# Moving GpSimd's share of the layer normalisation to other periods, with statistics in two places

## The reference

```python
xn = _layernorm(x, axis=-1)
# attention on xn
Q = jnp.einsum('bnd,hdk->bhnk', x, proj_q)
K = jnp.einsum('bmd,dk->bmk', x, proj_k)
V = jnp.einsum('bmd,dv->bmv', x, proj_v)
logits = jnp.einsum('bhnk,bmk->bhnm', Q, K)
weights = jax.nn.softmax(logits, axis=-1)
O = jnp.einsum('bhnm,bmv->bhnv', weights, V)
Y = jnp.einsum('bhnv,hdv->bnd', O, proj_o)
# feed-forward on xn, summed over 8 experts: (xn @ w1[e]) @ w2[e]
x = x + Y + ffn
```

## Time and profile before

| | |
|---|---|
| median of 3 runs | 1669.72 us (1669.16 to 1669.86) |
| the profiled execution's own time | 1669.67 us |
| its span, first to last instruction | 1667.9 us |
| TensorE busy | 1634.7 us, 98% |
| ScalarE, VectorE busy | 1304.2 us (78%), 1239.3 us (74%) |
| GpSimd busy | 1379.9 us, 83% |
| mean granted clock of TensorE | 0.998 of full speed |
| bytes moved by DMA | 16.73 MB, mean 10 GB/s |

### The profile page before, as it was taken

The page is one execution under the profiler, slowest core; times in us unless marked ns, Lnnn a source line. Parts: engine busy times, 40 slices in busy tenths (PEclk is TensorE's granted clock), DMA queues, the critical chain, the costliest instruction groups (busy, mean ns, idle before and its releaser), DMA issues.

```text
span 1667.9 us, 46510 instructions
## 1 busy us (share of the span) xinstructions
PE 1634.7 (98%) x18820; PEld 1214.1 (73%) x18820; DVE 1239.3 (74%) x2655; ACT 1304.2 (78%) x1350; POOL 1379.9 (83%) x1008
## 2 busy tenths in 40 slices
PE   7999999999999999999999999999999999999998
PEld 6777777777777777777777777777777777777775
DVE  5777777777777777777777777777777777777775
ACT  4777877787787788778778777877878787787785
POOL 2788888888888888888888888888888888878876
PEclk9999999999999999999999999999999999999999
DMA  8000000000000000000000000000000000000000
GB/s 230 2 2 2 1 2 14 2 2 2 2 15 2 2 2 3 13 2 2 2 8 8 2 2 1 8 8 2 2 2 8 8 2 2 2 14 2 2 1 14
DMA packets 16769, 16.73 MB, mean 10 GB/s; under 512 B 432, under 2 KB 12976, under 8 KB 16560
## 3 DMA queue, kind: packets, MB, share of 16 engines
q1 hardware_dynamic: 15520, 13.24, 2.7%
q10 hardware_dynamic: 1040, 0.52, 0.1%
HBM read 9.57 MB, written 4.19 MB: 8 GB/s over the span
## 4 chain that ended last, share of the span: by engine, by line
POOL 56%; issue 24%; PE 18%; ACT 1%; DVE 0%; POOLq 0%; DMA 0%; SPq 0%; DVEq 0%; ACTq 0%
POOL pr_lo L306 40%; POOL xacc L318 9%; POOL xn L300 3%; PE s_ps L548 2%; PE s_ps L550 2%; PE s_ps L535 2%; PE t_ps L586 2%; PE t_ps L589 2%; PE t_ps L588 2%; POOL rstd L345 2%; POOL xacc L324 1%; POOL xn_lo L290 1%; PE s_ps L432 1%; PE s_ps L434 1%; PE s_ps L433 1%
## 5 line engine op out<-in xcount | busy, mean ns | idle before, releaser
L306 POOL TENSOR_TENSOR pr_lo<-pr,pr_hi 128x1024 f16<-128x1024 f32 x511 | 1086.4, 2134 | 264.3 <-ACT pr_hi L396 264.3
L389 ACT ACTIVATE pr<-s_ps,boost,scale 128x1024 f32<-128x1024 f32 x512 | 616.8, 1205 | 211.1 <-PE s_ps L550 210.3
L778 DVE TENSOR_REDUCE key_max<-s_ps 128x128 f16<-128x1024 f32 x512 | 624.0, 1219 | 0.0
L396 ACT ACTIVATE pr_hi<-pr 128x1024 f16<-128x1024 f32 x512 | 525.4, 1051 | 8.1
L548 PE MATMUL s_ps<-g_lo,xT 128*128 128x128 f16 x4096 | 512.4, 219 | 1.1 <-DVE g_lo L791 1.1
L550 PE MATMUL s_ps<-g_hi,xT 128*128 128x128 f16 x4096 | 512.3, 219 | 0.0
L548 PEld LDWEIGHTS s_ps<-g_lo,xT 128*128 128x128 f16 x4096 | 400.7, 98 | 31.6 <-DVE g_lo L791 1.6
L550 PEld LDWEIGHTS s_ps<-g_hi,xT 128*128 128x128 f16 x4096 | 400.8, 98 | 29.7
L586 PE MATMUL t_ps<-pr_hi,xn_hi 128*128 128x512 f16 x1024 | 388.7, 380 | 16.3 <-POOL pr_lo L306 14.4
L588 PE MATMUL t_ps<-pr_lo,xn_hi 128*128 128x512 f16 x1024 | 388.1, 379 | 0.0
L589 PE MATMUL t_ps<-pr_hi,xn_lo 128*128 128x512 f16 x1024 | 388.1, 379 | 0.0
(11 more groups left out here) (123 smaller groups left out, 1602.7 us busy)
## 6 DMA issues: line engine op xcount, KB each, us to landing
out_dram<-xacc SPq DMA_DIRECT2D x16, 256.0 KB, 2.3
w_sb<-in_L_ffn_w_dram SPq DMA_DIRECT2D x1, 2048.0 KB, 10.2
pr<-in_L_attn_proj_q_dram ACTq DMA_DIRECT2D x1, 512.0 KB, 4.7
xacc<-in_L_attn_x_dram SPq DMA_DIRECT2D x2, 256.0 KB, 5.1
pr<-in_L_attn_proj_o_dram SPq DMA_DIRECT2D x1, 512.0 KB, 6.5
xacc<-in_L_attn_x_dram SPq DMA_DIRECT2D x1, 384.0 KB, 11.0
xacc<-in_L_attn_x_dram SPq DMA_DIRECT2D x1, 128.0 KB, 6.3
wkv<-in_L_attn_proj_k_dram SPq DMA_DIRECT2D x1, 64.0 KB, 2.9
```

Source lines behind the costliest of these rows:

```text
L306: pool.tensor_tensor(pr_lo[:, u % RING, :], pr32[:, u % PR, :], pr_hi[:, u % RING, :], ALU.subtract)\
L389: act.activation(pr32[:, u % PR, :], both_banks(u), ACT.Exp, bias=boost[:, 0:1], scale=scale[:, 0:1])\
L396: act.activation(pr_hi[:, u % RING, :], pr32[:, u % PR, :], ACT.Copy).then_inc(p_hi_ready, 1)
L778: dve.tensor_reduce(key_max[:, u % 2, :], both_banks(u).rearrange("p (t q) -> p q t", q=P), AX_X, ALU.max).then_inc(keys_max, 1)
```

## The change

The statistics get two slots, used in turn by even and odd tiles (`ln_slot`). VectorE's three steps stay in periods 0, 1 and 3 of pair p for tile p + 10. GpSimd and ScalarE now do their steps for that tile one pair later, in pair p + 1: `pow` in period 0 (before: 2), the normalisation in period 1 (before: 3), the high half on ScalarE in period 3 (before: 6), the low half in period 5 (before: 7). VectorE's wait before `bn_aggr` is for one normalised tile less. When TensorE turns the tile is unchanged.

```diff
@@ sizes: AHEAD + 1 becomes AHEAD + 2 for stats, mean_var, var_eps, rstd @@
+        def ln_slot(tile):
+            return AHEAD + tile % 2
...
@@ GpSimd @@
-                pool.tensor_scalar(xn32[:, 0, 1:D], xacc[:, tile, 1:D], mean_var[:, AHEAD, 0:1],
-                                   rstd[:, AHEAD:AHEAD + 1], ALU.subtract, ALU.mult).then_inc(ln_xn32, 1)
+                slot = ln_slot(tile)
+                pool.tensor_scalar(xn32[:, 0, 1:D], xacc[:, tile, 1:D], mean_var[:, slot, 0:1],
+                                   rstd[:, slot:slot + 1], ALU.subtract, ALU.mult).then_inc(ln_xn32, 1)
...
-                if n % 8 == 2 and (tile := ln_tile(n // 8)) is not None:
-                    pool.wait_ge(ln_var, tile - AHEAD + len(FIRST_TILES) + 1)
-                    pool.tensor_tensor(rstd[:, AHEAD:AHEAD + 1], var_eps[:, AHEAD:AHEAD + 1],
-                                       minus_half[:, 0:1], ALU.pow).then_inc(ln_rstd, 1)
-                if n % 8 == 3 and (tile := ln_tile(n // 8)) is not None:
-                    normalise_next(tile)
-                if n % 8 == 7 and (tile := ln_tile(n // 8)) is not None:
-                    xn_low(tile, 0, 1)
+                if (tile := ln_tile(n // 8 - 1)) is not None:
+                    if n % 8 == 0:
+                        slot = ln_slot(tile)
+                        pool.wait_ge(ln_var, tile - AHEAD + len(FIRST_TILES) + 1)
+                        pool.tensor_tensor(rstd[:, slot:slot + 1], var_eps[:, slot:slot + 1], minus_half[:, 0:1], ALU.pow)\
+                            .then_inc(ln_rstd, 1)
+                    if n % 8 == 1:
+                        normalise_next(tile)
+                    if n % 8 == 5:
+                        xn_low(tile, 0, 1)
@@ ScalarE @@
-                if n % 8 == 6 and (tile := ln_tile(n // 8)) is not None:
+                if n % 8 == 3 and (tile := ln_tile(n // 8 - 1)) is not None:
                     split_high(tile, 0, 1)
@@ VectorE: bn_stats, bn_aggr and the addition of EPS use ln_slot(tile); and @@
-                    dve.wait_ge(ln_xn32, tile)
-                    tile_mean(AHEAD)
+                    dve.wait_ge(ln_xn32, tile - 1)
+                    tile_mean(ln_slot(tile))
```

More of the change, by code:

```diff
@@ L66, in attention_ffn @@
         xn32 = sb("xn32", [P, AHEAD, D], F32)
[L67 to L70, removed]
+        stats = sb("stats", [P, AHEAD + 2, 6], F32)
+        mean_var = sb("mean_var", [P, AHEAD + 2, 2], F32)
+        var_eps = sb("var_eps", [P, AHEAD + 2], F32)
+        rstd = sb("rstd", [P, AHEAD + 2], F32)
         minus_half = sb("minus_half", [P, AHEAD], F32)
@@ L861, in before_bias @@
                         dve.wait_ge(x_in[4], 16)
-                    dve.bn_stats(stats[:, AHEAD, :], xacc[:, tile, :]).then_inc(ln_stats, 1)
+                    dve.bn_stats(stats[:, ln_slot(tile), :], xacc[:, tile, :]).then_inc(ln_stats, 1)
                 if at == 1 and (tile := ln_tile(pair)) is not None:
                     dve.wait_ge(ln_stats, tile + 1)
-                    dve.wait_ge(ln_xn32, tile)
-                    tile_mean(AHEAD)
+                    dve.wait_ge(ln_xn32, tile - 1)
+                    tile_mean(ln_slot(tile))
                 if at == 3 and (tile := ln_tile(pair)) is not None:
                     dve.wait_ge(ln_mean, tile + 1)
-                    dve.tensor_scalar_add(var_eps[:, AHEAD:AHEAD + 1], mean_var[:, AHEAD, 1:2], EPS).then_inc(ln_var, 1)
+                    slot = ln_slot(tile)
+                    dve.tensor_scalar_add(var_eps[:, slot:slot + 1], mean_var[:, slot, 1:2], EPS).then_inc(ln_var, 1)
                 if n == 0:
```

## The result

The changed kernel takes 1690.97 us (median of 4 runs, 1690.51 to 1691.02) against 1669.44 us before in the same session: ratio 1.0129, 95% interval 1.0117 to 1.0141. It is 21.5 us slower; 1687.3 us was forecast, in a range of 1683.5 to 1692. The profiled execution took 1690.94 us, its span is 1689.2 us.

What follows compares the result with a forecast made beforehand. The prediction took TensorE's own work plus gaps from waiting on GpSimd to bound the kernel. Profiled 1669.67 us - 22.9 (stall gone) + 40.5 (late tile) = 1687.3 us, range 1683.5 to 1692.

Steps and rivals of the forecast that it cites:

- What bounds the kernel: TensorE's work plus gaps from GpSimd: 0.44 us stall at every second block's first product; floor 24.91 us per pair.
- `pow` to period 0: GpSimd, behind add_head: its 0.53 us fit in 2.26 us of remaining idle time and cost nothing.
- Normalisation to period 1: GpSimd, behind add_head: still delays the last low half by its 0.79 us; margin 0.08 to 0.11 us.
- First term: TensorE's stall on GpSimd's last low half, at a block's first product, goes: 52 x 0.44 = 22.9 us less.
- `split_high` to period 3: ScalarE, ahead of the exponential: its 0.30 us hidden in 0.96 us idle, some 0.1 us to spare; taken as 0.
- `xn_low` to period 5 of the next pair: GpSimd finishes the tile after TensorE wants to turn it: 0.75 us wait, 54 times, 40.5 us more.
- by a different amount: Sign of being wrong: line 648, TensorE's turn, waits other than about 0.75 us on GpSimd's xn_lo.
- still late: Rival: GpSimd's last low half exceeds the margin; 1692.5 us at 0.1 us past it, 1710 us without gain; 8%.
- the tile is in time: Rival: xn_lo is ready before TensorE's turn, so only the saving stands: 1646.8 us, faster by 1.4%; 6%.
- another engine: Rival: ScalarE's split delays the exponential until TensorE misses it; 5.4 us on top at 0.1 us per pair, 1693 us; 3%.
- the two cancel: Rival: TensorE's turn waits only some 0.42 us, the stall that goes, leaving 1669.7 us; 3%.

Runs made afterwards that it cites:

- low_in_4: Changed kernel with xn_low in period 4 instead of 5, nothing else: 1645.36 us, ratio 0.9859 to the kernel before.
- pow_more_in_0: low_in_4 plus one pow with unused result on GpSimd in period 0 of each pair: 1645.81 us, ratio 0.9861 to the kernel before.
- pow_more_in_2: low_in_4 plus one pow with unused result on GpSimd in period 2 of each pair: 1668.73 us, ratio 0.9998 to the kernel before.
- low_in_3: Changed kernel with xn_low in period 3 instead of 5, ahead of the last low half: 1661.59 us, ratio 0.9956 to the kernel before.
- wait_first: Changed kernel with TensorE's wait for the tile put ahead of its wait for the exponential: 1686.48 us, ratio 1.0105 to the kernel before.
- late_low_only: Changed kernel with pow and normalisation back in periods 2 and 3, ScalarE's split in period 5, xn_low still in 5: 1690.11 us, ratio 1.0127.
- ahead_11: Changed kernel with 11 tiles normalised at the start instead of 10, places within a pair as changed: 1645.98 us, ratio 0.9861.

## Why the prediction was right, point by point

*What bounds the kernel.* TensorE's gaps, at one place in a pair. Shown by `low_in_4`: with both stalls gone TensorE is busy for 900.00 us of 900, and a pair takes 24.91 us.

*`pow` to period 0.* Forecast: free, and its 0.53 us gone from the chain. Shown by the pair `pow_more_in_0` and `pow_more_in_2`.

*Normalisation to period 1.* Forecast: still in the chain, so that the margin is only 0.08 to 0.11 us. The profile after has 0.09. That a piece in the gapless stretch counts next to the last low half is shown by `low_in_3`, and that it counts with a low half between by `pow_more_in_2`. The normalisation's duration did not change with the place (825 ns on average against a median of 830), and it stayed well above the 457 ns of the two-input addition:

```profile
L305 POOL TENSOR_SCALAR xn<-xacc,mean_var,rstd 128x127 f32<-128x127 f32 x54 | 44.6, 825 | 0.0
...
L329 POOL TENSOR_TENSOR xacc<-xacc,ffn_tmp 128x128 f32<-128x128 f32 x64 | 29.2, 457 | 5.0
```

The Trainium skill, "GPSIMD Engine Reference", section 4.1, has one-input work at roughly line rate; with the normalisation at the addition's price or less, `low_in_3` would have had no wait. The measurement decides here, for this instruction. The prediction's "the trace says the contrary" is too wide, though. In the kernel before one plain copy of 128 columns, also with one input, took 289 ns, less than the addition's 460 ns:

```profile
L274 POOL COPY centre<-ident 128x128 f32<-128x128 f32 x1 | 0.3, 289 | 0.1
```

What sets the two apart was not tested; the normalisation does two operations, each with a value per row.

*First term, 52 x 0.44 = 22.9 us.* From the kernel before to `low_in_4` it is 1668.81 - 1645.36 = 23.5 us.

*`split_high` to period 3.* Forecast: it ends some 0.1 us ahead of the exponential. ScalarE's timeline of the changed kernel:

```profile
817.87 0.31 ACT L368 ACTIVATE xn_hi<-xn 128x127 f16<-128x127 f32 x1 [0.51 <-POOL xn L305]
818.32 1.20 ACT L397 ACTIVATE pr<-s_ps,boost,scale 128x1024 f32<-128x1024 f32 x1
```

ScalarE waits 0.51 us for the normalisation, which takes the place of idle time: 817.87 + 0.31 = 818.18, 0.14 us ahead of the exponential. That one starts 818.32 - 811.78 = 6.54 us behind the block's first product, as before (807.03 - 800.49).

*`xn_low` to period 5 of the next pair.* The deciding step. The count of the periods and the path (2.43 us to the low half of period 5, then 2.09, 0.69 and 0.43) came out: `xn_lo` ends 804.15 - 798.52 = 5.63 us behind the first product, and 5.64 was worked out. **The term that was mis-sized is the last one**, the 0.06 us from `xn_lo` to TensorE. It was taken from line 586, whose wait was carried by the weight load. The wait for the tile comes behind another wait in the code and became an instruction of its own, and there the release takes 0.15 us. So a turn costs 0.83 us instead of 0.75, 54 x 0.83 = 44.8 us instead of 40.5, and the sum 1669.67 - 22.9 + 44.8 = 1691.6 us, against 1690.94 measured. `wait_first` shows it: with the order of the two waits changed the time is 17.7 us above the kernel before of the same session, and the prediction's two terms make 40.5 - 22.9 = 17.6 us. With the first term as `low_in_4` measured it (23.5 us) the sum is 1691.0 us.

*How far the number was luck.* The path was right, but the prediction bounded the turn's wait by 0.68 to 0.80 us and the time that follows by 1690 us; both were passed (0.83 us, 1690.97 us), and by its own words a wait "by a different amount" was a sign of being wrong. The time lies inside the range because that was widened to 1692 us for "still late", a rival that did not happen.

*That the two terms add with opposite signs* held because both were counted from the same natural schedule. Counted by itself from the kernel before, the late tile would have looked like 0.38 us at the turn, since the first stall hides the rest (`late_low_only`).

Of the rivals, "the tile is in time" is what `low_in_4` and `ahead_11` are; "still late" and "another engine" did not happen; "the two cancel" would have needed a turn that is 0.4 us late.

## What to carry to other kernels

When a step is moved in a pipeline of several engines, look for who uses its result and compare times in the trace, not loop indices: GpSimd finished the tile in its period 5 at 804.15, 0.68 us after TensorE, in its period 8, was ready to turn it (803.47). Of a stretch without gaps ask only whether a piece is in it or in the idle time outside: here the place within it made no difference. And two stalls on one chain must be counted from the schedule without stalls, since the first hides part of the second.

## What the runs showed of the hardware

A semaphore wait on TensorE that was an instruction by itself (54 turns of the changed kernel) released the matmul behind it 0.15 us after the releasing GpSimd instruction ended; carried by the weight load (54 turns of `wait_first`) it took 0.06 us. Each against the kernel before of its own session, the exchange of the two waits took 21.5 us of loss to 17.7 us: some 3.9 us, or 0.07 us for each of 54 waits, with an uncertainty of some 3 us by the two intervals; in the traces the turn comes 0.09 us earlier. Of the two waits ahead of the turn, the one that comes first in the code was the one carried, in both orders. The Trainium skill, "Perfetto Trace Analysis", section "Identifying Dependency Chains", says that instructions that wait on multiple engines may have EventSemaphore instructions ahead of them; the trace agrees: the turn waits on ScalarE and GpSimd, and one of the two waits stood by itself ahead of it.
